# Expert loads of a mixture-of-experts layer sent in one train per expert

## What is computed

```python
xb = jnp.zeros((E, CAP + 1, H), x.dtype).at[flat_e, pos_c].set(x[tok])   # E = 48, H = 512
xb = xb[:, :CAP]
gu = jnp.einsum('ech,eoh->eco', xb, gate_up_proj)                        # 2 x 192 columns
g, u = jnp.split(gu, 2, axis=-1)
h = jax.nn.silu(g) * u
out = jnp.einsum('eci,ehi->ech', h, down_proj)
y = out[flat_e, jnp.minimum(pos_c, CAP - 1)]
final = jnp.zeros_like(x).at[tok].add(y * w[:, None])
```

## Time and profile before

| | us |
|---|---|
| median of three runs | 1086.99 |
| the profiled execution | 1082.65 |
| its span, first to last instruction | 1080.9 |
| expert part, from the first scatter-add (704.27) to the end | 376.6 |
| mean granted TensorE clock, as a share of full | 0.988 |

### The profile page before, as it was taken

The page is one execution under the profiler, slowest core; times in us unless marked ns, Lnnn a source line. Parts: engine busy times, 40 slices in busy tenths (PEclk is TensorE's granted clock), DMA queues, the critical chain, the costliest instruction groups (busy, mean ns, idle before and its releaser), DMA issues.

```text
span 1080.9 us, 24325 instructions
## 1 busy us (share of the span) xinstructions
PE 1020.4 (94%) x6564; PEld 830.6 (77%) x6564; DVE 832.9 (77%) x2255; ACT 625.6 (58%) x1751; POOL 579.1 (54%) x565
## 2 busy tenths in 40 slices
PE   5999999999999999999999987999999999999993
PEld 3787778878878788778787875788888787877882
DVE  5678778878888788788887865588888878778782
ACT  4555455455455554554555541477767676676772
POOL 3224665676666666766666666434444343443444
PEclk9999999999999999999999999999999999999997
DMA  7999674543313112122134132489999999989984
GB/s 285 370 294 265 248 262 158 212 153 129 131 56 99 49 54 92 49 81 65 49 97 166 55 122 79 135 234 257 239 248 234 239 235 230 247 217 238 240 203 58
DMA packets 90644, 185.75 MB, mean 172 GB/s; under 512 B 23943, under 2 KB 24071, under 8 KB 89712
## 3 DMA queue, kind: packets, MB, share of 16 engines
q1 hardware_dynamic: 59232, 145.13, 41.2%
q0 software_dynamic: 31376, 40.20, 18.0%
HBM read 116.04 MB, written 122.00 MB: 220 GB/s over the span
## 4 chain that ended last, share of the span: by engine, by line
PE 52%; DMA 27%; issue 10%; POOL 5%; DVE 3%; ACT 1%; SPq 0%; POOLq 0%; DVEq 0%
PE ps L1226 27%; DMA layer_out<-qk_both,slot_table 22%; PE ps L1211 9%; PE ps L1216 4%; DMA arena<-in_x 4%; PE ps L1253 3%; PE ps L1324 2%; POOL layer_out L672 2%; PE ps L1357 2%; POOL slot_records L587 2%; PE ps L1382 2%; PE ps L1416 1%; DMA gu_sb<-in_weights 1%; POOL rstd L598 1%; DMA arena<-slot_records 1%
## 5 line engine op out<-in xcount | busy, mean ns | idle before, releaser
L587 POOL DMA_INDIRECT slot_records<-row,slot_idx x240 | 245.2, 1022 | 78.5 <-issue 50.0
L672 POOL DMA_INDIRECT layer_out<-qk_both,slot_table x96 | 161.6, 1683 | 223.2 <-DMA layer_out<-qk_both,slot_table 196.0
L598 POOL TENSOR_TENSOR rstd<-mv,neg_half 128x1 f32<-128x1 f32 x96 | 67.8, 707 | 121.4 <-DVE mv L966 78.5
L1226 PE MATMUL ps<-w_high,xn_high 128*128 128x512 f32 x384 | 114.1, 419 | 0.7 <-ACT xn_high L693 0.7
L728 ACT ACTIVATE arena<-ps,neg_max 128x128 f32<-128x128 f32 x256 | 90.1, 378 | 33.4 <-DVE neg_max L958 33.4
L1226 PE MATMUL ps<-w_low,xn_high 128*128 128x512 f32 x384 | 107.7, 403 | 0.0
L1226 PE MATMUL ps<-w_high,xn_low 128*128 128x512 f32 x384 | 106.7, 399 | 0.0
L1382 PE MATMUL ps<-w_high 128*128 128x192 f32 x576 | 89.7, 278 | 13.4 <-DVE w_low L1133 13.0
L1382 PEld LDWEIGHTS ps<-w_high 128*128 128x128 f32 x576 | 76.7, 191 | 30.2 <-issue 28.3
L1133 DVE TENSOR_TENSOR w_low<-gu_sb,w_high 128x1536 fp32r<-128x1536 f32 x48 | 84.4, 1758 | 16.1 <-ACT w_high L693 14.9
L693 ACT ACTIVATE xn_t<-ps 128x512 f32<-128x512 f32 x64 | 38.3, 599 | 98.9 <-PE ps L1211 98.8
(11 more groups left out here) (164 smaller groups left out, 2477.0 us busy)
## 6 DMA issues: line engine op xcount, KB each, us to landing
gu_sb<-in_gate_up SPq DMA_DIRECT2D x48, 768.0 KB, 5.9
slot_records<-arena SPq DMA_DIRECT2D x6, 3366.0 KB, 25.0
arena<-slot_records SPq DMA_DIRECT2D x48, 280.5 KB, 4.4
dn_sb<-in_down_proj SPq DMA_DIRECT2D x48, 256.0 KB, 3.7
arena<-in_x SPq DMA_DIRECT2D x32, 256.0 KB, 2.7
x_res<-in_x SPq DMA_DIRECT2D x32, 256.0 KB, 3.0
ctx_t_sb<-in_ctx_t SPq DMA_DIRECT2D x32, 256.0 KB
ctx_sb<-in_ctx_rows SPq DMA_DIRECT2D x32, 256.0 KB
```

The lines of the kernel that those rows point to most:

```text
L587: pool.indirect_dma_start(out=records, out_offset=bass.IndirectOffsetOnAxis(ap=slot_idx_of(s)[:, k:k + 1], axis=0), in_=row_of(s), in_offs ...
L598: pool.tensor_tensor(rstd[:, :], mv[:, 1:2], neg_half[:, 0:1], ALU.pow).then_inc(steps.sem, 1)
L672: pool.indirect_dma_start(out=out, out_offset=bass.IndirectOffsetOnAxis(ap=slot_table[0:PART[h], 2 * d.index + h:2 * d.index + h + 1], axi ...
L1226: last = pe.matmul(dst, left[:, c, :], right[:, m, c, :], start=(n == 0 and c == 0), stop=(n == 2 and c == KC - 1))
```

## The change

SP's loop waits for the low gate-up weights of expert k and then issues, one behind the other, the rows of k + 1, the gate-up weights of k + 2 and the down weights of k. The waits ahead of the single loads stay in the code. Ahead of the loop the gate-up weights of experts 2 and 3 and the rows of expert 2 go out.

```diff
+            def split_done(k):
+                sp.wait_ge(wgu_v.sem, wgu_v.after(k, "low"))
             load_gate_up(Batch(1, 0, E))
+            load_gate_up(Batch(1, 1, E))
+            load_rows(Batch(1, 0, E))
             with sp.Fori(1, E // 2 - 1) as pair:
                 for off in range(2):
-                    load_rows(Batch(pair, off, E))
-                    load_gate_up(Batch(pair, off + 1, E))
-                    load_down(Batch(pair, off, E))
-            load_rows(Batch(E // 2 - 1, 0, E))
-            load_gate_up(Batch(E // 2 - 1, 1, E))
+                    k = Batch(pair, off, E)
+                    split_done(k)
+                    load_rows(k.next())
+                    load_gate_up(k.next().next())
+                    load_down(k)
+            split_done(Batch(E // 2 - 1, 0, E))
+            load_rows(Batch(E // 2 - 1, 1, E))
             load_down(Batch(E // 2 - 1, 0, E))
-            load_rows(Batch(E // 2 - 1, 1, E))
             load_down(Batch(E // 2 - 1, 1, E))
```

## The result

The change makes the kernel slower: 1107.71 us (median of five runs, 1106.67 to 1109.93) against 1086.99, a ratio of 1.0194 with a 95% interval of 1.018 to 1.0208. The profiled execution took 1109.93 us with a span of 1108.2, 27.3 more than the span before. That is more than the 20.7 us between the medians, because the profiled execution before was a short one of its runs and this one a long one of its own.

What follows compares the result with a forecast made beforehand. The scatter-add was taken to bound the expert part; its beat falling from 7.90 to 7.6 us saves 11.1 us over 37 experts, less 1.0 at the loop's entry: 10.1 us, so 1077 us, range 1065 to 1100.

Steps and rivals of the forecast that it cites:

- The bound: Expert part: POOL's scatter-add sets the beat from 757 us on, 7.90 us an expert, and the other engines follow.
- its 1.5 us: Scatter-add: loads cost it 1.5 us, since it takes 7.90 us with them and 6.37 at the end without.
- rival (c): Expert part: scatter-add's first data wait behind a whole gate-up load every other turn; beat 8.28 us, 1102 us; chance 0.22.
- Both queues together run at 69.8 + 35.1 = 104.9%: Scatter-add: both queues' work adds up, so y0-to-y1 data take 4.4 to 4.8 us against 5.0, gaining 0.2 to 0.6.
- the place of the train: SP's loads each turn: rows move to 5.5 us behind a landing, down to 7.7; 2.74 us run without scatter-add data.
- the forecast's middle: Scatter-add: the middle gain of 0.4 us would bring the beat from 7.90 to 7.5; 7.6 was taken.
- costs no engine anything: SP's added wait for the low gate-up weights: no cost to any engine, since SP has nothing else to do.
- The entry of the loop: Loop start: expert 2's rows go behind expert 3's gate-up load; cost between nothing and 3.1 us, taken as 1.0.
- The two floors: Expert part's beat: PE's own 7.33 us, and 7.52 us for the DMA work at an engine share of 0.975.
- Rival (d): PE's transposes: rows come too late and stall PE 1.8 us, some 45 us in all; chance 0.07.

Runs made afterwards that it cites:

- e1: The change, with each gate-up load issued as four loads of 192 KB; 1086.54 us, 0.9991 of the kernel before.
- e10: The change, with each gate-up load issued as two loads of 384 KB; 1090.12 us, 1.0031 of the kernel before.
- e2: The change, with the gate-up load issued last, behind the rows and the down load; 1095.1 us, 1.0066 of the kernel before.
- e6: The change, with one more wait ahead of the rows of k + 1: until the scatter-add of expert k - 4 has landed; 1169.19 us, 1.075 of the kernel before.
- e4: The change without its added wait: rows go out as before, only the down load stays behind the gate-up load; 1088.35 us, 1.0003 of the kernel before.
- e9: The kernel before, with the gate-up load held until the scatter-add on its way has landed; ratio 1.0414.
- e5: The kernel before, with the gate-up load held until the low rows of the same expert are made; ratio 0.9983.
- e8: The kernel before, with each gate-up load issued as two loads of 384 KB; 1086.26 us, 0.9978 of the kernel before.

## Why the prediction was wrong

**What held.** The bound was read rightly: the expert part's beat is the scatter-add's. The loads that stood ahead of y1 did cost it its 1.5 us: with them away, in the odd turns, the data time is 3.59 us against 5.05. The forecast of rival (c), with its place, its mechanism and the alternation of a blocked and a clear turn, is what happened: it gave a beat of 8.28 and 1102 us, which was outside the stated range of 1065 to 1100, and it became 8.54 and 1107.7. The clear turns run at 6.39 and not at PE's 7.33, and the blocked ones at 10.68 and not 9.23, since a blocked one gets two trains.

**The step that failed** is the one in which the gain was worked out: "Both queues together run at 69.8 + 35.1 = 104.9%", so that the work of both adds up and the span of y's data is their sum over 1.05, 4.4 to 4.8 us against 5.0. Counted from the point at which the first data are due to the last, the mean span was 5.05 us before and became 5.72 (1.35 of wait and 4.37 of data). The rows that the 1.05 came from the earlier trace rows have down and rows loads against y1, loads of 280.5 KB and less. Against a gate-up load that came first the queues did not share: the first data stood still for 2.68 us past their due in the mean even turn. The earlier trace rows showed that already, in 2 us without a row of q0. I counted it as a rare event when it came in every other turn, and the sum itself put 1.8 to 2.2 us of the train at just that meeting. By that row the forecast should have gone to (c).

The rule that stood beside (c), from the Trainium skill (the page "DMA: Bandwidth & Descriptors", section "Queues, rings and completion order": an engine changes from one queue to the other only when a packet is drained), agrees with e1, e10 and the change, where the wait shrinks with the size of the load in front. No run here shows what a packet is for these loads, so e2 and e6 are not settled by it.

**The second error** is the place of the train. I let it start against a landing 7.74 us after the last, 2.4 us ahead of it. When the turn becomes short, the landing comes forward and the train's release does not: it hangs on the low weights, 5.3 us behind the landing before. So the better the scatter-add does in one turn, the worse it meets the train in the next. The sum had 1.84 to 2.24 us of the train's work within the span; it was 5.2 in an even turn and 0.3 in an odd one, 2.75 on the mean, and 2.42 before. With what really ran there (2.65 and 2.75) the sum over 1.05 gives 5.1 us: about half of the miss against the 4.6 of the forecast's middle is this term, the other half the standing still. Before the change the same locking helped: the gate-up load, released by the low weights, used the 2.74 us behind a landing in which the scatter-add moves no data.

**A third** is that SP's wait "costs no engine anything". No engine waits for SP, but e4, which leaves out that wait alone, is back at 1.0003 of the time before: the wait costs by where it puts the rows, and behind them the gate-up load.

**Smaller terms.** The entry of the loop was put at 1.0 us; it cost none: PE starts the transposes of expert 2 at 701.67, right behind the products, without the 1.51 us of the earlier trace rows. The two floors, 7.33 and 7.52, were not reached by the change. Rival (d), rows too late, did not come about (0.6 us of PE's waits in 240).

**The accounts.** Of the 27.3 us between the two profiles, 0.8 lie ahead of the first scatter-add (705.06 against 704.27; this execution's first stage was 2.6 us longer, and the entry 1.8 shorter), 1.0 in the first six turns (52.24 against 51.20), 22.4 in the next 36, 3.3 from there to the last expert's first instruction (36.21 against 32.88), and the rest is 0.2 shorter.

## What to carry to other kernels

Here a 768 KB load that was under way when a smaller transfer of another queue came due kept it out, 2.68 us in the mean even turn of the change. Where such a transfer sets the beat, look at when its data become ready, not at how busy the engines are, and see that the large load is through by then. Cutting the load in four took the loss away. Releasing it by the other transfer's landing did not: the two runs that did so, e9 and e6, are the slowest, since the load then falls on the next data. And check what the release hangs on once the beat itself has changed.

## What was not expected of the hardware

The cost of the meeting sets in late and then fast. On the mean of the 36 turns the kernel before issues the gate-up load 2.67 us ahead of a landing. Holding it back to 1.00 us ahead (e5) cost nothing that can be told, with a wait of 0.17 us for the first data; holding it back by one us more, to 0.03 us behind the landing (e9), cost 4.1% of the whole time, with a wait of 1.03 us. And smaller pieces take the engines hardly more time: by q1's share from 760 to 1000 and the beat, an expert's loads take 4.84 us of the engines in the change (56.7%), 4.85 in two pieces (e10, 60.8%) and 4.91 in four (e1, 62.7%); in the kernel before it is 4.61 whole and 4.61 in two pieces (e8, 58.4%).
